# Moving the first group of exponentials, the copy of transposed q and the next layer's row transposes inside the first attention layer of a two-layer decoder

## What is computed

```
x = x + L0_attn(layernorm(x))
# L0_attn
qkv = x.reshape(-1, 512) @ weight_qkv.T          # 16 query heads, 4 key and value heads of 32
q = q.transpose(1, 2, 0, 3)                      # attention runs over the 16 sequences' axis
scores = einsum('bhqd,bhkd->bhqk', q, k) * scale # scale = 1/sqrt(32)
scores = where(causal, scores, -inf)
probs = softmax(scores, axis=-1)
attn = einsum('bhqk,bhkd->bhqd', probs, v)
out = attn @ weight_proj.T
# then, for the next layer:
x = x + L0_xattn(layernorm(x), ctx, ...)         # its input is normalised twice, scaled and rounded to fp8
```

## Time and profile before

| | |
|---|---|
| median of 3 runs | 4108.85 us (4096.33, 4108.85, 4111.47) |
| the profiled execution | 4103.33 us, its span 4101.6 us |
| first attention, from the first full projection to the last rounding | about 36 to 384 us of the span |
| TensorE busy, whole span | 3556.4 us, 87% |
| VectorE, ScalarE, GpSimd busy | 2466.7 us (60%), 1643.2 us (40%), 807.8 us (20%) |
| mean granted TensorE clock, whole span | 0.934 of full speed |

### The profile page before, as it was taken

One profiled execution on the slowest core, in us unless ns is written; L12 is line 12 of the kernel. 1 busy time (PEld: TensorE's weight loads), 2 busy tenths in 40 slices (PEclk: granted clock), 3 DMA queues, 4 the chain that ended last, 5 costly groups with the idle time before them and its releaser, 6 DMA issues. The chain is left out here.

```text
span 4101.6 us, 55851 instructions
## 1 busy us (share of the span) xinstructions
PE 3556.4 (87%) x18548; PEld 2849.7 (69%) x18548; DVE 2466.7 (60%) x6496; ACT 1643.2 (40%) x3680; POOL 807.8 (20%) x909
## 2 busy tenths in 40 slices
PE   6893699599599999959999987999679979997999
PEld 4773577477477777747777765888557756665887
DVE  3766588488566666656666657899555642225533
ACT  4543344344243343333343432788233433332222
POOL 1222244144222222212222223000322210000000
PEclk9876799799799999989999998999889989998999
DMA  4002200100200000020000005999520004332100
GB/s 157 14 11 67 57 0 0 62 0 0 80 25 18 25 18 25 9 88 19 25 18 25 26 0 206 349 400 404 161 78 1 1 21 132 109 105 99 33 9 18
DMA packets 86516, 296.74 MB, mean 72 GB/s; under 512 B 9104, under 2 KB 15248, under 8 KB 81120
## 3 DMA queue, kind: packets, MB, share of 16 engines
q1 hardware_dynamic: 79968, 276.45, 19.0%
q0 software_dynamic: 6400, 18.36, 1.5%
HBM read 252.57 MB, written 42.21 MB: 72 GB/s over the span
## 5 line engine op out<-in xcount | busy, mean ns | idle before, releaser
L39 PE MATMUL bank<-cross_w,cross_ctx_part 128*125 128x512 f32 x2304 | 593.9, 409 | 11.7 <-DVE cross_qn L883 7.3
L39 PEld LDWEIGHTS bank<-cross_w,cross_ctx_part 128*125 128x125 f32 x2304 | 425.4, 186 | 134.2 <-DVE cross_qn L883 9.2
L39 PE MATMUL bank<-self_w,self_xq 128*112 128x512 f32 x1024 | 268.9, 411 | 94.4 <-ACT self_xq L780 94.4
L889 DVE TENSOR_REDUCE cross_neg_max<-bank 112x1 f32<-112x375 f32 x256 | 133.1, 530 | 295.7 <-PE bank L699 293.0
L39 PEld LDWEIGHTS bank<-self_w,self_xq 128*112 128x112 f32 x1024 | 177.6, 181 | 146.6 <-ACT self_xq L780 95.2
L815 ACT ACTIVATE cross_prob<-bank,cross_neg_max 112x375 f32<-112x375 f32 x256 | 147.1, 575 | 323.5 <-DVE cross_neg_max L889 323.5
L39 PE MATMUL bank<-moe_wt,moe_zT 128*128 128x448 f32 x1176 | 267.1, 377 | 2.1 <-DVE moe_zT L1460 1.5
L1455 DVE TENSOR_TENSOR moe_wt<-moe_raw,moe_wt 128x1792 fp32r<-128x1792 f32 (+1 forms) x111 | 231.8, 2109 | 14.5 <-ACT moe_wt L1362 11.1
L39 PEld LDWEIGHTS bank<-moe_wt,moe_zT 128*128 128x128 f32 x1176 | 217.3, 191 | 18.3 <-issue 1.7
L39 PE MATMUL bank<-mlp_zT,mlp_signs 128*128 128x448 f32 x1024 | 221.1, 369 | 4.7 <-DVE mlp_zT L2069 4.7
L39 PEld LDWEIGHTS bank<-mlp_zT,mlp_signs 128*128 128x128 f32 x1024 | 193.8, 190 | 26.5 <-issue 5.0
(11 more groups left out here) (389 smaller groups left out, 7713.8 us busy)
## 6 DMA issues: line engine op xcount, KB each, us to landing
moe_raw<-in_moe_w SPq DMA_DIRECT2D x74, 896.0 KB, 7.6
moe_raw<-in_moe_w SPq DMA_DIRECT2D x37, 1024.0 KB, 8.4
stream<-in_L1f SPq DMA_DIRECT2D x32, 768.0 KB, 4.4
cross_ctx_raw<-in_ctxT SPq DMA_DIRECT2D x32, 750.0 KB, 4.2
wide_ctxT<-in_ctxT SPq DMA_DIRECT2D x16, 750.0 KB, 12.7
wide_ctx_rows<-in_ctx SPq DMA_DIRECT2D x16, 750.0 KB
expert_rows<-a_zeros SPq DMA_DIRECT2D x1, 8960.0 KB, 26.5
moe_zrow<-expert_rows SPq DMA_DIRECT2D x35, 256.0 KB
```

Source lines behind the costliest of these rows:

```text
L39: mm = pe.matmul(out, a, b, start=first and n == 0, stop=last and n == len(pairs) - 1)
L889: dve.tensor_reduce(neg_max[:, HS * t:HS * (t + 1)], score_bank(t)[0:S, 0:HS * NK].rearrange("p (h n) -> p h n", h=HS), AX.X, ALU.max, neg ...
```

## The change

Three moves in `first_layer`; no instruction is added or removed.

- ScalarE: `exponential(t, 0)` stands ahead of `take_q(t+1)`.
- ScalarE: `take_turned` is split; the copy of transposed q (`take_qT`) stands between `exponential(t, 2)` and `exponential(t, 3)`, the copy of transposed k (`take_kT`) stays behind `exponential(t, 3)`.
- TensorE: `transpose_z2(t-2)` stands between the transposes of probability group 0 and those of groups 1 to 3, ahead of the weighing, and ScalarE's `take_z2T(t-2)` stands between the copies of group 0 and group 1.

```diff
-            def transpose_probs(t):
-                for r in range(4):
+            def transpose_probs(t, rows):
+                for r in rows:
@@
-                transpose_probs(t)
-                weigh_values(t)
+                transpose_probs(t, (0,))
                 if t >= 2:
                     transpose_z2(t - 2)
+                transpose_probs(t, (1, 2, 3))
+                weigh_values(t)
                 if t + 2 < NT:
                     transpose_z(t + 2)
@@
-            def take_turned(t):
+            def take_qT(t):
                 act.wait_ge(s["qT_in_psum"], t + 1)
                 act.activation(qT[:], tiled(6), ACT.Copy).then_inc(s["q_ready"], 1)
+
+            def take_kT(t):
                 act.wait_ge(s["kT_in_psum"], t + 1)
                 act.activation(kT[:], ps[4][:, 0:T], ACT.Copy).then_inc(s["k_ready"], 1)
@@
+                exponential(t, 0)
                 if t + 1 < NT:
                     take_q(t + 1)
-                exponential(t, 0)
                 exponential(t, 1)
                 if t + 1 < NT:
                     take_kv(t + 1)
                 exponential(t, 2)
+                if t + 1 < NT:
+                    take_qT(t + 1)
                 exponential(t, 3)
                 if t + 1 < NT:
-                    take_turned(t + 1)
-                for r in range(4):
-                    take_probsT(t, r)
+                    take_kT(t + 1)
+                take_probsT(t, 0)
                 if t >= 2:
                     take_z2T(t - 2)
+                for r in range(1, 4):
+                    take_probsT(t, r)
```

More of the change, by code:

```diff
@@ L2469, in _ @@
             take_kv(0)
-            take_turned(0)
+            take_qT(0)
+            take_kT(0)
             z_high(1)
```

## The result

The changed kernel takes 4079.43 us (median of 5 runs, 4069.54 to 4088.87) against 4108.85 us before (median of 5, 4096.33 to 4112.85): a ratio of 0.9932, 95% interval 0.9906 to 0.9957, so 0.7% faster. The forecast was 4074 us with a range of 4058 to 4095. The total came out as forecast; the terms of the sum did not, and the larger finding lies there. Of all runs reported here one, of e4, took 4133.19 us at a granted clock of 0.875 and is left out; the others had 0.929 to 0.943.

A forecast was written before the change was run, and what follows sets the result against it. Two things bound the first attention: a chain of waits through all engines and TensorE's clock. Path -17.8 + 9.5 - 12.7 = -21.0 us and clock -8 gave -29 from 4103.3: 4074 us, range 4058 to 4095.

The forecast's parts named there:

- Exponentials ahead of the copy of q: ScalarE's first four exponentials fit its wait for q: -1.37 us in 13 iterations, -17.8 us.
- the copy of q isn't late: The moved exponentials run from about 146.3 to 147.7, inside ScalarE's 2.14 us wait for q, so the gain is whole.
- The copy of transposed q: Moved among the exponentials, counted 0; it lets the z2 transposes start, else they delay group 1 by 0.65 us.
- `take_z2T` between copies: Group 3's transposes wait for group 1's copy, now behind `take_z2T`: +0.79 us in 12 iterations, +9.5 us.
- From the weighing to the maxima: Weighing's end to the next `tops`: 3.9 us instead of 5.12, -12.7 us over the iterations.
- the lower bound: Low end of the time from the weighing to the next maxima: 3.5 us, against 4.3 at the high end.
- The sum of the path: First attention's chain of waits: -17.8 + 9.5 - 12.7 = -21.0 us, by its ends -14 to -27.
- I take 8 of 19.2 us: Clock term: -8 us in the total, of 19.2 us lost to six half-speed weighings in the first attention.
- the forecast's own signs of being wrong: More half-speed weighings, over 2 us of gap before group 3, or ScalarE waiting before copies of v, transposed q or k.
- the forecast 355: End of the first attention stage expected at about 355 us instead of 384.
- speaking against recovery: The new gap of 1.35 us was named against all the lost clock coming back (4063 us, chance 0.09).
- Rival 4: Clock falls every iteration from the gap between groups 2 and 3 to the scores: slower, 4127 us; chance 0.05.

The follow-up runs named there:

- e4: Changed kernel plus three extra 512-column matmuls ahead of the wait of probability group 3: 4057.97 us, ratio 0.9885 to the kernel before.
- e1: Kernel before with only the first four exponentials moved ahead of the copy of q: 4057.55 us, ratio 0.9879.
- e6: Kernel before plus three extra 512-column matmuls ahead of the wait of probability group 3: 4096.76 us, ratio 0.9930.
- e11: Kernel before with two groups of four exponentials ahead of the copy of q, nothing else moved: 4081.17 us, ratio 0.9907.
- e7: Changed kernel with the copy of transposed q back behind the last exponentials: 4090.22 us, ratio 0.9915 to the kernel before.
- e3: Changed kernel with ScalarE's copy of transposed z2 behind all four copies of probabilities: 4055.09 us, ratio 0.9878 to the kernel before.
- e10: Kernel before with only the first exponentials ahead of the copy of q, run again on the repeated changed kernel's chip: 4069.82 us, ratio 0.9876.
- e8: Changed kernel with both the late copy of z2 and three extra matmuls ahead of group 3's wait: 4054.42 us, ratio 0.9826 to the kernel before.
- e9: Changed kernel, unchanged, measured and profiled again in another set: 4102.73 us, ratio 0.9951 to the kernel before.
- e5: Kernel before, unchanged, run for a second profile: 4129.86 us (one run).
- set 1: The follow-up runs e1, e3, e4 and one of the z2 move alone, measured on one chip; kernel before there: 4107.3 us.

## Why the prediction was right, and where not

**Exponentials ahead of the copy of q: right in the idle, too large on the path.** Forecast 1.37 us less idle in front of group 1, measured 1.39 (2.12 to 0.73, e1); the wait for q fell from 2.14 to 0.78. The forecast then counted the whole 1.37 us in 13 iterations, since "the copy of q isn't late". That was read off t = 5, where the projection starts with the maxima (145.42 and 145.38). At full clock TensorE is ahead: in e6 the projection starts at 168.52, the maxima at 169.97. The moved exponentials still have to wait for those maxima, and q, which e6 takes 1.60 us after them, is taken 2.49 us after them in e1 (84.11 - 81.62). From the maxima to group 1 it is 178.84 - 169.97 = 8.87 us in e6 and 89.97 - 81.62 = 8.35 us in e1: only 0.52 of the 1.37 us is left. Whether one group is the right number e11 doesn't settle.

**The copy of transposed q: right about its role.** Without it the transposes of `z2` wait 0.49 us and group 1 comes 0.25 us later (e7), where the forecast said 0.65. No effect on the total could be measured.

**`take_z2T` between copies: right mechanism, size too small.** Forecast +0.79 us, measured 1.25 - 0.29 = +0.96 us in front of group 3.

**From the weighing to the maxima: the size was off where it counts.** Forecast 3.9 us instead of 5.12. At full clock it is shorter still, 3.50 us as the lower bound said, where e1 has 4.90: in the changed kernel the weighing's last issue ends at 249.09 and these maxima start at 252.59.

```profile
249.09 0.63 PE L2315 MATMUL bank<-ident,a_z 128*128 128x128 f32 x4
...
252.59 2.48 DVE L2516 TENSOR_REDUCE a_neg_max<-bank 128x4 f32<-128x512 f32 x4
```

At half clock it is 4.89 us: TensorE's transposes, masks and scores take 207.03 to 211.85. Six iterations in a row of the changed kernel have 4.4 to 4.9 us.

**The sum of the path** was forecast at -21 us. At full clock an iteration of the old order takes 19.29 us in e6, of which the filling is 0.2 (from group 1 to group 3 it has 1.60 us instead of the 1.40 of the earlier trace rows), so 19.1; in the new order 18.10 in e4 and 0.09 more without its filling, so 18.2. That is 0.9 us less, some -11 us in 12 iterations. The same measure splits it: the exponentials alone bring 19.1 to 18.6 (e1), all three moves 18.2, all with a late copy 17.26 (e3). So the move of `z2` is not a loss on the path: at full clock it saves 1.40 us behind the weighing and costs 0.96 in front of group 3, as the forecast had it in kind, and with its copy behind the others it would save nearly 1.4. The mis-sized term is that of the exponentials: -0.5 us in an iteration where the sum has -1.37.

What is left above these full-clock iterations can be put down to the clock. The estimate below takes the eleven iterations from the maxima of tile 2 to those of tile 13 in VectorE's timeline and subtracts eleven times the iteration at full clock; it is rough, since the last iterations do a little less work.

| kernel | eleven iterations, us | one at full clock, us | left for the clock, us |
|---|---|---|---|
| before, first and second profile | 246.7, 259.7 | 19.1 | 37, 50 |
| before, gap filled (e6) | 232.3 | 19.3 | 20 |
| changed, first and second profile | 231.4, 237.3 | 18.2 | 31, 37 |
| exponentials only (e1, e10) | 210.5, 210.7 | 18.6 | 6, 6 |
| changed, late copy (e3) | 208.2 | 17.3 | 18 |
| changed, gap filled (e4) | 207.4 | 18.1 | 8 |
| late copy and filled (e8) | 191.6 | 17.4 | 1 |

By this estimate the kernel with one move beats that with all three by the clock alone: its path is 4 to 5 us longer, and it pays 25 to 31 us less for the clock.

**The clock: the step that failed.** "I take 8 of 19.2 us" rested on one execution in which half the iterations happened to run fast. Against that first profile the change brought 2 to 5 us of clock back (13.2 us in the stage, 11 of them path, or 15.3 in the eleven iterations, 10 of them path). Against the second, in which nearly all take 24.0 us, it brought 12 to 18 (50 less 31 to 37). The second is nearer the usual case: the medians of the kernel before in the three sets, less the 1.8 us outside the span and what the profiles of each set took behind the stage, put its end at 397 to 408 us (an estimate), where the first profile had 384.4. The medians fell by 29.4 us and 24.5 us (e9). So the nearness of the total is in part luck: the path gave half of its -21, the clock about twice its -8 from the usual case, and of the 24.0 us between the two profiles 10.8 came from behind the stage.

One of the forecast's own signs of being wrong came: weighings of over 5 us are eight in the changed kernel's profile and six in the first of before. Each is shorter, 5.2 to 6.0 us but for the first (6.87), where those of before take 6.88; in e5 they are twelve. The stage also ended at 371 us instead of the forecast 355.

**What the gap ahead of the weighing costs the clock was the finding that the sum left out.** e4 and e6 add work and shorten next to nothing, and win 20 and 28 us. The gap of 1.25 us, told in the prediction as speaking against recovery, costs about twice the 0.96 us by which it had grown: closing it (e3) or filling it (e4) brings the stage to about 350 us either way; of e3's 22.6 us about half is path, in e4 nearly all is clock. Rival 4 had its place right (half clock from the gap through masks and scores, iterations of 21.7 to 22.7 us) but not its weight, since the kernel before paid at least as much for its clock.

On the page "TensorE: Matmul & The Clock Gate" of the Trainium skill, section "Part 4: PE-mode transpose": its rule that transposes don't count as busy in the same way isn't refuted. Filling the gap with transposes of `z2` left the clock at 0.84 to 0.85 (before 0.80 to 0.85); filling it with 512-column matmuls gave 0.90 to 0.91. But e3 holds full clock for five iterations with those same transposes in the gap and 0.6 us of idle, and the kernels differ in more than the kind of matmul, so a clean test of the rule wasn't made.

**Open:** how the clock follows from the order of work in one iteration. That the idle ahead of the weighing costs clock is shown by filling it (e4, e6) and by closing it (e3). That the few columns of the weighing's matmuls have a part in it was never varied. Why e1, with transposes of `z2` behind the weighing and 0.73 us of idle in front of group 1, holds 0.91 and e3 0.86 was not settled.

## What to carry to other kernels

Where a chain of waits and TensorE's clock both act, take at least two profiles of the kernel before: here two of one program differed by 20 us in a stage that ends at about 400. Test each move of a change by itself; here one of three gave more than all three, and putting one small copy back behind those that a bank waited for (e3) won that loss back. Measure an iteration between two of the same event on the engine that closes the chain: from mask to mask e1 looks 1 us faster than it is. Where the clock is low in short stretches, try to fill the idle with harmless wide matmuls: it costs three instructions in an iteration and says at once how much the clock is worth.

## What the runs showed of the hardware

- Added matmuls made the program faster: 42 of them (0.81 us for three in e4) took the kernel before, in e6, from 4124.3 to 4096.8 us.
- The same 32 weighing matmuls took 3.66 us at full clock and 6.88 us at half, in two executions in which the same waits of 2.1 and 0.29 us stood ahead of them.
- One program's first attention ended at 384.4 us in one execution and at 404.4 us in another.
- The part of the kernel behind it took 3703 to 3708 us in the profiles of one chip (set 1) and 3717 to 3726 us in those of two others.
